# Packed gelu and gating, DMA-filled planes, and a gate convolution woven into the local attention, in a two-stage convolution kernel

## What is computed

```python
xn = ln_last(x, ln1_g, ln1_b)                      # stage 1, per image
q, k, v = [conv3x3(conv1x1(xn, a), b) for a, b in ((q1, q3), (k1, k3), (v1, v3))]
probs = softmax(k^T q / scale, per head)
x1 = conv1x1(v probs, o_w) + x
xn = ln_last(x1, ln2_g, ln2_b)
gate = gelu(conv3x3(conv1x1(xn, g1), g3))          # 64 channels
info = conv3x3(conv1x1(xn, i1), i3)                # 64 channels
x2 = conv1x1(gate * info, r1) + x1
out = leaky(instance_norm(conv3x3(x2, conv1_w)))   # stage 2
out1, mask = conv3x3(out, conv2_w), sigmoid(conv3x3(out, mask_w))
q, k, v = conv1x1 of out * mask
out2 = softmax over the 3x3 neighbours (q . k), applied to v
y = x2 + out1 * mask + (1 - mask) * out2
```

## Time and profile before

| | before |
|---|---|
| runs (us) | 219.03, 218.00, 218.53; median 218.53 |
| profiled execution (us) | 216.99, of which 215.2 is the span from first to last instruction |
| PE busy | 184.4 us, 86% of the span |
| PE weight load busy | 106.9 us, 50% |
| DVE busy | 174.9 us, 81% |
| ACT busy | 123.5 us, 57% |
| POOL busy | 70.1 us, 33% |
| mean granted PE clock | 0.988 |

### The profile page before, as it was taken

The page is one execution under the profiler, slowest core; times in us unless marked ns, Lnnn a source line. Parts: engine busy times, 40 slices in busy tenths (PEclk is TensorE's granted clock), DMA queues, the critical chain, the costliest instruction groups (busy, mean ns, idle before and its releaser), DMA issues. The chain is left out here.

```text
span 215.2 us, 5212 instructions
## 1 busy us (share of the span) xinstructions
PE 184.4 (86%) x2063; PEld 106.9 (50%) x2071; DVE 174.9 (81%) x403; ACT 123.5 (57%) x258; POOL 70.1 (33%) x62
## 2 busy tenths in 40 slices
PE   2699889699977998999879788999699997899882
PEld 2268268234346454744637345744324444576651
DVE  7897999989657997899798995999949677983582
ACT  2284444645282864929765474656945684876750
POOL 7603405050402221830029211850044018430290
PEclk9999999979999999999999999999999999999998
DMA  6421041003400000001000200000000000000002
...
DMA packets 9193, 5.95 MB, mean 28 GB/s; under 512 B 7056, under 2 KB 7536, under 8 KB 9168
## 3 DMA queue, kind: packets, MB, share of 16 engines
...
...
## 5 line engine op out<-in xcount | busy, mean ns | idle before, releaser
L1439 PE MATMUL ps<-sh_ln,w_gi 96*128 96x512 f32 x96 | 44.8, 618 | 1.7 <-DVE sh_ln L316 1.7
L461 POOL TENSOR_TENSOR ln_s<-ln_s,neg_half 128x16 f32<-128x16 f32 x7 | 20.4, 2920 | 57.7 <-DVE ln_s L922 57.7
L583 ACT ACTIVATE sh_ln<-ln_out 32x512 f32<-32x512 f32 (+2 forms) x49 | 27.5, 562 | 14.0 <-DVE ln_out L943 7.2
L1439 PEld LDWEIGHTS ps<-sh_ln,w_gi 96*128 96x128 f32 x96 | 18.2, 196 | 23.8 <-issue 23.6
L1482 PE MATMUL ps<-sh_in,w_in 96*32 96x256 f32 x384 | 22.5, 381 | 1.3 <-DVE sh_in L316 1.3
L1387 PE MATMUL ps<-w_qk,sh_ln 128*128 128x128 f32 x192 | 23.2, 278 | 0.4 <-issue 0.4
L1387 PEld LDWEIGHTS ps<-w_qk,sh_ln 128*128 128x128 f32 x192 | 22.2, 192 | 1.9 <-DMA sh_ln<-ln_out 0.9
L1353 PE MATMUL ps<-busy 128*128 128x512 bf16 x69 | 18.6, 402 | 1.3 <-issue 0.6
L486 POOL TENSOR_TENSOR omm<-ones,msk 128x512 f32<-128x512 f32 x4 | 7.1, 1780 | 33.6 <-DVE msk L1142 33.6
L1482 PEld LDWEIGHTS ps<-sh_in,w_in 96*32 96x32 f32 x384 | 11.7, 110 | 11.6 <-DVE sh_in L316 2.6
L316 DVE COPY sh_in<-act_c 32x496 f32<-32x496 f32 (+1 forms) x28 | 15.7, 562 | 0.5
...
## 6 DMA issues: line engine op xcount, KB each, us to landing
...
```

The lines of the kernel that those rows point to most:

```text
L461: nc.gpsimd.tensor_tensor(ln_s[n][:, 3, :], ln_s[n][:, 2, :], neg_half[:, :], ALU.pow)\
L583: return nc.scalar.activation(o, i, ACT.Copy)
L1439: mm = nc.tensor.matmul(ps[:, GI_BANKS[n], :], w_gi[:, dy, :, :].rearrange("p m o -> p (m o)"), xs[:, n // 2, y:y + H // 2, 0:W], start=(d ...
```

## The change

1. `gate_info` puts the two halves of an image into the two halves of the partitions of one bank, and gate and info into different banks: instead of one product of 96 x 128 columns it runs two of 96 x 64 columns, the first into partitions 0-63, the second into 64-127. So `gelu` and `gated` work on 128 partitions, two of each for a pair instead of four; the signals count 2.
2. For pairs 1 to 3, slot 1 of sh_ln2 is filled by four DMAs of 64 KB from SP (`ln2_planes`), not by three copies on DVE and one on ACT.
3. The last part of the second norm of pair 1 (ln_apply, three slot-0 copies, three slot-2 copies) moves from step 0 into the prologue.
4. The copy of v out of PSUM in the two steps moves from DVE to ACT (`v_evac`).
5. On PE the three fills around `window_q` and `window_k` (2 + 4 + 3 products in step 0, 5 + 4 in step 1) go, and the rows dy = 0, 1, 2 of the gate bank n = 0 of the next pair are computed there; so PE waits for the planes of the next pair ahead of `window_q`, not behind `window_v`. In step 1 the third row stands between `window_scores` and `window_v`.
6. On POOL, `residual` is split: `complement` (1 - mask) first, the rest later; `final(0)` waits until DVE has made the planes of step 1, and `residual(2)` runs behind the weights and the planes of pair 3.

```diff
@@ -383,6 +383,15 @@
+            def ln2_planes(pair):
+                ln2_planes_free(sp, pair)
+                sp.wait_ge(g_ln[1].sem, g_ln[1].done(pair))
+                for r in range(R):
+                    at = (1 + RH * r) * W
+                    sp.dma_start(sh_ln2[pair % 2][C:2 * C, :, at:at + BLK], ln2_out[C * r:C * r + C, :, :])\
+                      .then_inc(planes_by["ln2"]["dma"].sem, 16)
             def halo(pair):
...
@@ -416,9 +425,12 @@
                 load_res(pair + 2)
+                ln2_planes(pair + 1)
                 halo(pair)
                     ln1_planes(pair + 3)
+                else:
+                    ln2_planes(pair + 2)
                 store(pair)
...
@@ -477,13 +489,17 @@
-            def residual(pair):
+            def complement(pair):
                 nc.gpsimd.tensor_tensor(omm[pair % 2][:, :], ones[:, :], msk[:, :], ALU.subtract).then_inc(g.sem, 1)
+            def residual(pair):
+                g = g_res
                 pool.wait_ge(g_o1.sem, g_o1.done(pair))
...
@@ -506,13 +522,19 @@
+            def in_planes_copied(pair):
+                pool.wait_ge(planes_by["in"]["dve"].sem, planes_by["in"]["dve"].done(pair))
             def step(pair, norm):
+                complement(pair)
                 residual(pair)
                     scaled_weights(pair + 1)
+                    in_planes_copied(pair + 1)
                     final(pair, pair)
...
@@ -552,9 +574,12 @@
             but_last, last = PAIRS - 2, PAIRS - 1
-            residual(but_last)
+            complement(but_last)
             inorm_rstd(last)
             scaled_weights(last)
+            in_planes_copied(last)
+            residual(but_last)
+            complement(last)
             residual(last)
...
@@ -612,10 +637,10 @@
-            def gelu(pair, n):
-                act.wait_ge(g_i.sem, g_i.at(pair, n + 1))
+            def gelu(pair, i):
+                act.wait_ge(g_i.sem, g_i.at(pair, 2 * i + 1))
                 act.wait_ge(g_gi.sem, g_gi.before(pair))
-                nc.scalar.activation(gate[EC:P, n, :], ps[0:EC, GI_BANKS[n], :], ACT.Gelu).then_inc(g_gelu.sem, 1)
+                nc.scalar.activation(gate[:, i, :], ps[:, GI_BANKS[2 * i], :], ACT.Gelu).then_inc(g_gelu.sem, 1)
...
@@ -635,7 +660,8 @@
                 act.wait_ge(g_xm.sem, g_xm.before(pair))
-                act.wait_ge(g_res.sem, g_res.before(pair))
+                if not is_first(pair):
+                    act.wait_ge(g_res.sem, g_res.at(pair - 1, 1))
                 nc.scalar.activation(th[:, :], ps[:, mask_bank(early), :], ACT.Tanh, bias=half_bm[:, 0:1], scale=0.5)\
...
@@ -705,7 +731,7 @@
             def ln2_planes(pair):
-                ln2_copies(pair, [(1, R - 1)] + [(2, r) for r in range(R)], done=True)
+                ln2_copies(pair, ([(1, R - 1)] if is_first(pair) else []) + [(2, r) for r in range(R)], done=True)
...
@@ -715,14 +741,19 @@
                 load_exp_table()
-                if not is_first(pair):
+                if is_first(pair):
+                    ln2_copies(1, [(2, r) for r in range(3)])
+                else:
                     squares(1, pair + 1)
                 v4_evac(pair + 2)
-                ln2_planes(pair + 1)
+                if is_first(pair):
+                    ln2_copies(1, [(2, 3)], done=True)
+                else:
+                    ln2_planes(pair + 1)
                 tanh_mask(pair)
...
@@ -734,17 +765,15 @@
                 window_exp(pair)
+                v_evac(pair)
                 gelu(pair + 1, 0)
-                gelu(pair + 1, 1)
                 if norm:
                     ln1_planes(pair + 3)
-                    gelu(pair + 1, 2)
-                    gelu(pair + 1, 3)
+                    gelu(pair + 1, 1)
                 else:
-                    ln2_copies(pair + 2, [(1, R - 1), (2, 0)])
-                    gelu(pair + 1, 2)
+                    ln2_copies(pair + 2, [(2, 0)])
+                    gelu(pair + 1, 1)
                     ln2_copies(pair + 2, [(2, 1), (2, 2)])
-                    gelu(pair + 1, 3)
                     ln2_copies(pair + 2, [(2, 3)], done=True)
...
@@ -1050,13 +1075,15 @@
                 ln_apply(1, ln2_out, "ln2", pair)
-                ln2_copies(pair, [(1, r) for r in range(R - 1)] + [(0, r) for r in range(R)], done=True)
-            def gated(pair, n):
-                dve.wait_ge(g_gelu.sem, g_gelu.at(pair, n + 1))
+                ln2_copies(pair, ([(1, r) for r in range(R - 1)] if is_first(pair) else []) + [(0, r) for r in range(R)],
+                           done=True)
+            def gated(pair, i):
+                dve.wait_ge(g_gelu.sem, g_gelu.at(pair, i + 1))
+                dve.wait_ge(g_i.sem, g_i.at(pair, 2 * i + 2))
                 dve.wait_ge(g_r1.sem, g_r1.before(pair))
-                nc.vector.tensor_tensor(gi[EC * (n % 2):EC * (n % 2) + EC, n // 2, :], ps[EC:P, GI_BANKS[n], :],
-                                        gate[EC:P, n, :], ALU.mult).then_inc(g_gi.sem, 1)
+                nc.vector.tensor_tensor(gi[:, i, :], ps[:, GI_BANKS[2 * i + 1], :],
+                                        gate[:, i, :], ALU.mult).then_inc(g_gi.sem, 1)
...
@@ -1150,13 +1177,6 @@
-            def v_evac(pair):
-                dve.wait_ge(g_v.sem, g_v.done(pair))
-                dve.wait_ge(g_pv.sem, g_pv.before(pair))
-                for h in range(2):
-                    nc.vector.tensor_copy(v_t[:, 4 * h:4 * h + 4, :].rearrange("p u m -> p (u m)"),
-                                          ps[:, (7, 4)[h], :]).then_inc(g_v_sb.sem, 1)
             def window_softmax(pair, early=False):
...
@@ -1221,7 +1241,10 @@
                 head_scores(pair + 2)
-                ln2_apply(pair + 1)
+                if is_first(pair):
+                    ln2_copies(1, [(0, 3)], done=True)
+                else:
+                    ln2_apply(pair + 1)
                 scaled_act(pair)
...
@@ -1232,22 +1255,16 @@
                 ln_var(*((0, pair + 3) if norm else (1, pair + 2)))
-                v_evac(pair)
                 window_probs(pair)
                     gated(pair + 1, 1)
-                    gated(pair + 1, 2)
-                    gated(pair + 1, 3)
                 else:
                     gated(pair + 1, 0)
+                    ln2_copies(pair + 2, [(0, 0)])
                     gated(pair + 1, 1)
-                    ln2_copies(pair + 2, [(1, r) for r in range(R - 1)])
-                    gated(pair + 1, 2)
-                    ln2_copies(pair + 2, [(0, 0)])
-                    gated(pair + 1, 3)
                     ln2_copies(pair + 2, [(0, 1), (0, 2), (0, 3)], done=True)
...
@@ -1286,27 +1303,25 @@
             ln1_apply(2)
+            ln2_center(1)
             gated(0, 0)
-            ln2_center(1)
+            ln_var(1, 1)
             gated(0, 1)
-            gated(0, 2)
-            ln_var(1, 1)
-            gated(0, 3)
             x2_all(0)
+            ln_apply(1, ln2_out, "ln2", 1)
+            ln2_copies(1, [(0, r) for r in range(3)])
             step(0, True)
             but_last, last = PAIRS - 2, PAIRS - 1
-            gated(last, 0)
             inorm(but_last)
             in_planes(but_last)
+            gated(last, 0)
+            scaled_act(but_last)
             gated(last, 1)
-            gated(last, 2)
-            scaled_act(but_last)
-            gated(last, 3)
             x2_all(last)
...
@@ -1435,18 +1450,12 @@
                 for dy in rows:
-                    y = H // 2 * (n % 2) + dy
-                    mm = nc.tensor.matmul(ps[:, GI_BANKS[n], :], w_gi[:, dy, :, :].rearrange("p m o -> p (m o)"),
-                                          xs[:, n // 2, y:y + H // 2, 0:W], start=(dy == 0), stop=(dy == 2))
+                    for h in range(2):
+                        y = H // 2 * h + dy
+                        mm = nc.tensor.matmul(ps[EC * h:EC * h + EC, GI_BANKS[n], :], w_gi[:, dy, n % 2, :],
+                                              xs[:, n // 2, y:y + H // 2, 0:W], start=(dy == 0), stop=(dy == 2))
                 if 2 in rows:
                     mm.then_inc(g_i.sem, 1)
-            def gate_info_all(pair, bank_3_read_of):
-                planes_ready("ln2", pair)
-                gate_info(pair, 0)
-                pe.wait_ge(g_x1.sem, g_x1.done(bank_3_read_of))
-                for n in range(1, 4):
-                    gate_info(pair, n)
...
@@ -1588,16 +1597,23 @@
                 front_read(pair + 2)
-                stay_busy(2 if norm else 5, 5)
+                planes_ready("ln2", pair + 1)
+                gate_info(pair + 1, 0, (0,))
                 window_q(pair)
-                window_k(pair, busy_for=4)
+                gate_info(pair + 1, 0, (1,))
+                window_k(pair)
                 if norm:
-                    stay_busy(3, 2)
+                    gate_info(pair + 1, 0, (2,))
                 else:
                 window_scores(pair)
+                if not norm:
```

(6 more changed lines are left out.)

16 lines of the change are left out of this document (6 added, 10 removed).

## The result

Before 218.53 us, changed kernel 212.76 us (median of 4 runs); ratio 0.9715, 95% interval 0.9673 to 0.9757. Forecast 212.0, range 209 to 216. The profiled execution of the changed kernel took 212.97 us, 4.02 less than the 216.99 of the one before.

The account below looks back on a forecast made before the run. No engine alone bounds the kernel; DVE sets the end of step 0, and PE counts where continuous. Lead 5.6 + 0.9 for code gaps = 6.5 off 216.99 gives 210.5, with the offset 212.0; range 209.0 to 216.0.

Parts of the forecast that it names:

- Gate convolution: On PE, a round of two 64-column products in different array halves takes 0.90 us, bounds 0.88 to 1.76.
- rival 1: The array halves do not overlap: up to 0.88 us on each of 48 rounds, time about 250; chance 0.05.
- Prologue: Before step 0: the last gelu leaves the path, +0.5, twelve gate rounds cost 0.25; rows start 0.2 us earlier (lead 0.2).
- Step 0: Fewer gate rounds behind window_v and less DVE work: lead 2.4 us at conv1(1), with ACT's p_t late next.
- Step 1, front: final(0) waits for the planes: DVE copies 2.5 us less, lead 3.6 at mask_conv, second norm lengthened by 1.4.
- The DMAs of slot 1: Pair 2's four plane DMAs land at 124.4, PE ready at 123.7 waits ahead of the gate row; lead 3.4 at window_q.
- Step 1, back: From the scores to conv1(2): nine rounds behind window_v, ACT's p_t late last; lead 5.8 us at conv1(2).
- rival 2: The granted PE clock falls behind waits: one to three falls at 1.5 to 2 us each, 214 to 217; chance 0.1.
- a sign of being wrong: The prediction is wrong if the clock row shows stretches under 1 in the steps.
- Epilogue and end: Nine rounds cost 0.2, lead 5.6; two code gaps in the scores of pairs 2 and 3 give 0.9 of 1.7.
- rival 4: Code gaps in the scores of pairs 2 and 3 all go: 5.6 + 1.7 = 7.3, 211.2; chance 0.15.
- The offset of 1.54: The median before lies 1.54 us above its profiled execution; the same was expected after, 210.5 becoming 212.0.

Follow-up runs that it names:

- run 4: Changed kernel with PE's order of before: fills around window_q and window_k, all gate rows of the bank behind window_v; 212.31 us.
- run 9: Changed kernel with v's copy back on DVE, ahead of the window probabilities; 215.47 us.
- run 7: Kernel before with only POOL's final(0) held until DVE has copied the seven parts of sh_in in step 1; 217.82 us.
- run 3: Changed kernel with SP reordered: load_res(3) at the end of step 0, store(0) behind pair 2's four plane DMAs; 211.66 us.
- run 11: Changed kernel with run 3's SP order, four fills ahead of the wait for pair 2's planes and nine behind reduce_1(2); 210.19 us.
- run 12: Run 11 with two slot-2 plane copies of pair 3 moved from ACT to DVE, and four fills instead of nine behind reduce_1(2); 208.82 us.
- run 6: Kernel before with only the 64-column gate products and gelu and gating on 128 partitions, one execution for its trace; 214.97 us.
- run 8: Kernel before with 78 tiny products (156 PE instructions) ahead of PE's first fills, to move the places of the code; 219.2 us.
- run 1: Changed kernel again, no edit, to see how much it varies; 212.35 us.
- run 2: Changed kernel plus five fill products in step 1 between conv2 and the wait for pair 2's planes; 212.06 us.
- run 10: Changed kernel with slot 1 of pair 2 filled by DVE and ACT copies, not by DMA; 213.45 us.

## Why the prediction held, step by step

**Gate convolution.** Taken at 0.90 us a round, measured 0.88. The group of these products in the changed kernel (busy us, mean ns | idle time ahead and what ended it):

```profile
L1455 PE MATMUL ps<-sh_ln,w_gi 96*64 96x512 f32 x192 | 46.6, 625 | 3.3 <-DVE sh_ln L316 1.7
```

Nine rounds in a row (18 products, 36 instructions) took 7.92 us, 0.88 each. The halves of the array overlap fully (rival 1 falls). A single round between 128-column products takes 1.01 us (80.87 to 81.88 in the changed kernel), so the changes of shape cost 0.13, as forecast. The Trainium skill (TensorEngine Tiling (Array Packing), Key Properties) says that a change of tiling mode drains the array; the rows agree.

**Prologue.** Lead 0.21 against 0.2, once the late load of the vectors is taken out.

**Step 0.** 2.20 against 2.2, and `p_t` on ACT is what ends last (0.30 us ahead of `window_out`), as the step said; but `reduce_1` waited 0.59 for DVE just before, so the two queues end close together. Undone one at a time, the weave costs 1.0 (run 4) and v's copy 1.1 (run 9).

**Step 1, front.** Copies in 3.39 us, no wait ahead of `mask_conv`, the norm lengthened by 1.4 (1.08 and 1.68, as in run 7): as forecast. Less the 1.56 us by which the vectors came late, the second norm is done at 120.1 (forecast 120.2) and conv2 at 123.4 (123.7).

**The DMAs of slot 1.** The mechanism was right and the size off: the wait is 1.55 us, 0.8 was forecast. The four issues take 0.63 each, as costed, but I let them begin at 120.4, right behind the norm; they begin at 122.22 - 1.56 = 120.66, 0.6 us behind its end, since the load ahead of them is itself 0.57 us and starts only behind the store, which waits for `final(0)`. The gate row starts at 126.49 - 1.56 = 124.93 (forecast 124.5), and PE is ready 0.3 us earlier than forecast. That the wait is the DMA's, run 3 shows.

**Step 1, back.** 3.07 at full clock against 3.4; the 0.33 missing fits the 0.43 by which the gate row is late; run 3, where the gate row came 0.44 earlier and `window_out` 0.42, shows that such a delay goes through. That ACT's `p_t` is late last is shown by runs 11 and 12.

**The clock.** This is the term that was left out of the sum: the mechanism of rival 2, at chance 0.1, took place, with one fall of 1.45 us (1.5 to 2 was its price) in the profiled execution, and by the mean clock in five of eight. The clock row reads under 1 in step 1, which the prediction had named as a sign of being wrong; the forecast held in spite of it. The time stayed under the 214 to 217 of that rival. The waits were also mis-sized, 0.8 and 1.3 us in the forecast, 1.55 and 2.30 in the trace; whether smaller ones would have kept the clock up is not shown.

**Epilogue and end.** -0.11 against -0.2. At the end 1.66 against 0.9: both gaps in the scores are gone, which is the case that rival 4 priced at 1.7. But the gaps alone would give half of that. In runs 6 and 8 they are gone too, for 0.77 and 0.79 us: the second gap is time, while PE, freed of the first, waits 1.04 us for DVE's planes of pair 3. In the changed kernel PE has no wait there (`mask_conv` starts 10.28 us behind conv1(3), 11.38 before, 11.36 in run 8). That is what the prediction said of `residual(2)` and the first gap, each worth nothing without the other; no run undoes POOL's order alone, so that this part of the edit brings the planes earlier is argued, not shown. The Trainium skill (Runtime: NRT & Kernel Launch, Instruction fetch mechanics) has such crossings mostly hidden. Most are here too (17 packets on that queue in the changed kernel, and no gap over 0.5 us without a releaser); the earlier trace rows and run 8 show where one is not: in a dense run of small products.

**The sum.** 0.21 + 2.20 + 1.62 - 0.11 + 1.66 = 5.58, with 6.5 forecast. The difference of 0.92 is the fall (1.45) and the back of step 1 (0.33), less the gaps (0.76) and 0.1 elsewhere. The medians differ by 5.77, near 5.58. The offset of 1.54 did not carry over (after, the median is 0.21 below the profiled execution): it belongs to single executions, through the load of the vectors and the falls of the clock, and not to the kernel. So that the forecast came within 0.8 us is partly luck: for the profiled execution it was 210.5, and 2.5 too low against 212.97 (1.56 of it the load of the vectors, 0.92 the steps), and the offset, added on top, was 1.75 too high.

**Left open.** Which wait is followed by a lower clock. Waits of 1.26 us (runs 8 and 9), 1.55 (the changed kernel), 1.74 (run 9), 2.29 (run 1) and 2.30 (runs 2 and 10) had one; waits of 1.26 (before), 1.45 (run 9), 1.49 (run 1), 1.97 (run 6), 2.30 (run 3) and 2.56 (run 9) had none. The wait of 1.72 to 1.74 us ahead of the first gate rows had one in ten of the thirteen traces read here, and none in runs 6, 7 and 8. The length of the wait alone does not tell, and the runs do not show what does. A fall cost from 1.45 to 4.98 us.
